# Pre-norm attention with level weights and a top-2 expert layer: two score groups of each head as one plain float32 product

## The reference

```
q = (x @ Wq.T).reshape(b, t, H, S)
k = (x @ Wk.T).reshape(b, t, H, S)
v = (x @ Wv.T).reshape(b, t, H, HD)
...
scores = jnp.einsum('bthd,bshd->bhts', q, k) * scale
...
A = scores * decay * lamw
y = jnp.einsum('bhts,bshd->bthd', A, v).reshape(b, t, H * HD)
out = y @ Wo.T + x
```

## Time and profile before

| what | value |
|---|---|
| median of three runs | 1522.22 us |
| the profiled execution's own time | 1523.29 us |
| its span, first to last instruction | 1521.5 us |
| TensorE busy | 1451.9 us, 95% |
| ScalarE busy | 1149.5 us, 76% |
| VectorE busy | 1013.6 us, 67% |
| GpSimd busy | 894.6 us, 59% |
| mean granted TensorE clock | 0.984 of full |

### The profile page before, as it was taken

How to read it: one execution, slowest core, us unless ns; L and a number is a source line. 1 busy time by engine, 2 the same in 40 slices (tenths; PEclk the granted TensorE clock), 3 DMA queues, 4 the chain that set the end, 5 groups by cost and what they waited for, 6 DMA issues and landing times.

```text
span 1521.5 us, 31013 instructions
## 1 busy us (share of the span) xinstructions
PE 1451.9 (95%) x10733; PEld 1198.0 (79%) x10733; DVE 1013.6 (67%) x2336; ACT 1149.5 (76%) x3379; POOL 894.6 (59%) x984
## 2 busy tenths in 40 slices
PE   5699999999999999999999999999999999999996
PEld 4488788878888788887888788887888878878873
DVE  5355756687656866577665876678766686657677
ACT  2588888787788778887787877888778877777730
POOL 2064558745596456945578455964569545685561
PEclk9699999999999999999999999999999999999998
DMA  6311111102010111101111011111111011111100
GB/s 186 63 11 17 40 17 31 14 16 48 9 37 17 23 38 38 17 8 38 25 38 14 16 36 18 38 17 23 38 38 16 9 26 21 39 17 17 23 8 15
DMA packets 256487, 44.14 MB, mean 29 GB/s; under 512 B 197976, under 2 KB 254666, under 8 KB 256202
## 3 DMA queue, kind: packets, MB, share of 16 engines
q1 hardware_dynamic: 255484, 41.90, 14.7%
q10 hardware_dynamic: 846, 0.25, 0.1%
HBM read 32.38 MB, written 9.18 MB: 27 GB/s over the span
## 4 chain that ended last, share of the span: by engine, by line
PE 61%; POOL 17%; DVE 9%; ACT 7%; issue 3%; SPq 1%; DMA 1%; ACTq 0%; POOLq 0%; DVEq 0%
PE o_ps L1344 16%; PE l_ps L1275 9%; POOL a_lo L603 7%; PE s_ps L1259 7%; PE s_ps L1261 6%; PE s_ps L1260 6%; PE aux L1259 5%; PE aux L1260 4%; PE aux L1261 4%; ACT w_all L727 3%; POOL e_rs L609 2%; DVE a_all L923 2%; POOL yn L628 2%; PE o_ps L1339 1%; POOL yn L638 1%
## 5 line engine op out<-in xcount | busy, mean ns | idle before, releaser
L603 POOL TENSOR_TENSOR a_lo<-a_all,a_hi 128x512 fp32r<-128x512 f32 (+2 forms) x640 | 710.8, 1127 | 561.0 <-ACT a_hi L749 560.3
L923 DVE TENSOR_TENSOR a_all<-s_ps,w_all 128x512 f32<-128x512 f32 (+3 forms) x768 | 421.8, 554 | 348.4 <-PE s_ps L1261 335.7
L727 ACT ACTIVATE w_all<-l_ps,bias 128x128 f32<-128x128 f32 x2304 | 628.9, 388 | 27.3 <-PE l_ps L1275 25.4
L749 ACT ACTIVATE a_hi<-a_all 128x512 fp32r<-128x512 f32 (+2 forms) x640 | 362.8, 598 | 210.2 <-DVE a_all L923 208.3
L1344 PE MATMUL o_ps<-a_hi,v_all 128*128 128x512 f32 (+2 forms) x1280 | 459.0, 363 | 7.2 <-POOL a_lo L603 7.2
L1259 PE MATMUL s_ps<-q_hi,xt_hi 128*128 128x512 f32 (+3 forms) x768 | 298.5, 389 | 9.5 <-DVE a_all L923 8.5
L1344 PEld LDWEIGHTS o_ps<-a_hi,v_all 128*128 128x128 f32 x1280 | 241.2, 188 | 45.5 <-issue 6.3
L1260 PE MATMUL s_ps<-q_lo,xt_hi 128*128 128x512 f32 (+3 forms) x768 | 266.5, 347 | 0.0
L1261 PE MATMUL s_ps<-q_hi,xt_lo 128*128 128x512 f32 (+3 forms) x768 | 266.4, 347 | 0.0
L1344 PE MATMUL o_ps<-a_lo,v_all 128*128 128x512 f32 (+2 forms) x640 | 230.0, 359 | 0.0
L1259 PEld LDWEIGHTS s_ps<-q_hi,xt_hi 128*128 128x128 f32 x768 | 145.7, 190 | 27.9 <-DVE a_all L923 19.8
(11 more groups left out here) (194 smaller groups left out, 2034.8 us busy)
## 6 DMA issues: line engine op xcount, KB each, us to landing
rb<-eb_scratch SPq DMA_DIRECT2D x1016, 0.8 KB
ra<-ea_scratch SPq DMA_DIRECT2D x512, 4.0 KB, 2.0
mt<-m_scratch SPq DMA_DIRECT2D x62, 128.0 KB, 2.1
nt<-n_scratch SPq DMA_DIRECT2D x62, 128.0 KB, 2.6
tx<-in_L_attn_x SPq DMA_DIRECT2D x9, 512.0 KB, 4.3
out<-yn SPq DMA_DIRECT2D x15, 256.0 KB, 2.8
yx<-in_L_attn_x SPq DMA_DIRECT2D x7, 512.0 KB, 4.2
ea_scratch<-tx SPq DMA_DIRECT2D x15, 128.0 KB
```

What stands on the lines that cost most here:

```text
L603: pool.tensor_tensor(a_lo[r][:, 0:t1 - t0], a[r][:, 0:t1 - t0], a_hi[r][:, 0:t1 - t0].bitcast(F32), ALU.subtract).then_inc(a_lo_done, 1)
L727: last = act.activation(w[k][:, W_AT[j] + dd, :].rearrange("p (f c) -> p f c", f=2), l_tiles[:, :, :, i - i0], ACT.Exp, bias=bias[b % 2][: ...
L749: act.activation(a_hi[r][:, 0:t1 - t0], a[r][:, 0:t1 - t0], ACT.Copy).then_inc(a_hi_done, 1)
L923: dve.tensor_tensor(a[(n * NG + g) % NA][:, 0:t1 - t0], s_ps[:, g % 2, 0:t1 - t0], w[n % 2][:, at:at + (t1 - t0) // P, :].rearrange("p i n ...
```

## The change

Groups 6 and 11 of each head, so 128 groups in all, are no longer three passes over split operands but one matmul of unsplit float32 tiles, as their values were already. For that, VectorE copies the last 128 columns of each half of the queries out of PSUM into `q_full`, between the two instructions of `take_q`, with a wait for its own copy. ScalarE copies the last 128 columns of each half of the transposed tokens into `x_full`, ahead of x_hi, and VectorE's `token_low` waits for that as well. The split tiles are still made for all columns. The size of one scratch area for DMA descriptors is set from 8192 to 4096 bytes.

```diff
+        q_full = [sb(f"q_full{k}", [P, 2 * P]) for k in range(2)]
+        x_full = [sb(f"x_full{k}", [P, 2 * P]) for k in range(2)]
...
+        q_full_done, x_full_done = sem("q_full_done"), sem("x_full_done")
...
                 def token_high(b, f):
...
                         act.wait_ge(y_done, 2 * (b - 1))
+                    act.activation(x_full[b % 2][:, f * P:(f + 1) * P], bank(("T", b, f))[:, HALF - P:],
+                                   ACT.Copy).then_inc(x_full_done, 1)
                     act.activation(xt_hi[b % 2][:, f * HALF:(f + 1) * HALF], bank(("T", b, f)), ACT.Copy).then_inc(t["hi"], 1)
...
                 def take_q(n, u):
...
                     dve.tensor_copy(q_hi[n % 2][:, cols], bank(piece)).then_inc(q_hi_done, 1)
                     dve.wait_ge(q_hi_done, Q_U * n + u + 1)
+                    dve.tensor_copy(q_full[n % 2][:, u * P:(u + 1) * P], bank(piece)[:, HALF - P:]).then_inc(q_full_done, 1)
+                    dve.wait_ge(q_full_done, Q_U * n + u + 1)
                     dve.tensor_tensor(q_lo[n % 2][:, cols], bank(piece), q_hi[n % 2][:, cols].bitcast(F32),
                                       ALU.subtract).then_inc(freed(piece), 1)
...
                 def token_low(b, f):
...
                     dve.wait_ge(t["hi"], 2 * b + f + 1)
+                    dve.wait_ge(x_full_done, 2 * b + f + 1)
...
                 def scores(n, g):
...
                     keys = slice(j * P, (j + 1) * P)
+                    if g in FULL:
+                        f = FULL.index(g)
+                        pe.matmul(s_ps[:, g % 2, 0:P], x_full[b % 2][:, f * P:(f + 1) * P],
+                                  q_full[k][:, f * P:(f + 1) * P], start=True, stop=True).then_inc(s_mm, 1)
+                        return
                     three(s_ps[:, g % 2, 0:t1 - t0], xt_hi[b % 2][:, keys], xt_lo[b % 2][:, keys],
                           q_hi[k][:, t0:t1], q_lo[k][:, t0:t1]).then_inc(s_mm, 1)
...
-    nc = bacc.Bacc("TRN2", target_bir_lowering=False, num_devices=1, dynamic_dma_scratch_size=8192)
+    nc = bacc.Bacc("TRN2", target_bir_lowering=False, num_devices=1, dynamic_dma_scratch_size=4096)
```

## The result

The changed kernel takes 1517.87 us (median of 13 runs, 1516.5 to 1519.85) against 1521.94 us for the kernel before (13 runs, 1520.55 to 1524.44). The ratio is 0.9976, with a 95% interval of 0.9967 to 0.9984: 4.1 us gained where 8 were forecast. The time lies inside the range of 1505 to 1521.5 us, but the gain is half of the forecast, so the account had a wrong term in it.

What follows compares the result with a forecast made beforehand. TensorE was taken to set the pace for some 60% of the time. 12.3 - 2.3 - 0.3 - 1.1 = 8.6 us off the profiled 1523.3 gave 1514.7, adjusted to the median as 1514 us against 1522.2, range 1505 to 1521.5.

Steps and rivals of the forecast that it cites:

- the size of the saving in a group: Groups 6 and 11 on TensorE: three narrow passes cost 0.41 us, the plain product 0.25, saving 0.16 (0.08 to 0.19).
- The range: Forecast time from 1505 to 1521.5 us, to reach the eaten gain and halfway to the case with every saving counted.
- the case where all counts: Rival: all 128 groups save 0.16 us, as GpSimd's and VectorE's work moves with TensorE; 1504 us, chance 0.10.
- 60% of the groups count: Only the 77 of 128 groups standing where TensorE sets the pace save time: 77 x 0.16 = 12.3 us.
- the fifth head's stretch: Part of each batch's chain paced by VectorE and ScalarE in turns, from 670.7 to 697.3 us: 26.6 us.
- The copies cost 2.3 + 0.3, with 1.1 for paths that come close: Seven exposed VectorE copies at 0.33 us, ScalarE's first at the start, and a tenth of the gain for new waits.
- The gain is eaten by waits: Rival: another 17 to 26 take_q exposed behind VectorE's copies lose 5.6 to 8.6 us; 1521 us, chance 0.16.
- VectorE becomes the bound: Rival: late q_lo holds its aux bank in every half head, all 126 copies exposed; 1552 us, chance 0.07.
- Four full passes: Rival: the plain float32 product costs four passes of 0.11 us, 0.50 a group instead of 0.41; 1533 us, chance 0.03.
- The scratch area: The smaller DMA descriptor scratch costs nothing; that it or something like it holds up loads had chance 0.02.
- The signs to look for: Trace: product 0.22 to 0.33 us, 128 copies near 285 ns, TensorE busy 15 to 20 us less, batch 178.1 us.
- the two signs of being wrong: TensorE's waits for take_q or weigh rising over 10 us, or the new product adding over 0.35 us to the chain.

Runs made afterwards that it cites:

- product_alone: The changed kernel without VectorE's 128-column copies for all heads but the first two, so later products read old queries: 1514.17 us, 0.9946 of the kernel before.
- copies_alone: The changed kernel with all copies made but groups 6 and 11 as three split passes again: 1526.56 us, 1.0025 of the kernel before.
- copy_twice: The changed kernel with VectorE's copy into q_full made twice over: 1530.74 us, 1.0050 of the kernel before.
- values_first: The changed kernel with the values of the group five back ahead of the scores in groups 6 and 11: 1520.05 us, 0.9981 of the kernel before.
- changed_again: The changed kernel itself, run again on another occasion beside the kernel before: 1519.13 us, ratio 0.9978.
- late_sum: The changed kernel with VectorE making q_full later, as q_hi + q_lo at places where it was idle, not inside take_q: 1516.38 us, 0.9962 of the kernel before.
- late_some: The changed kernel with q_full made later as q_hi + q_lo only for queries made in a batch's first and fifth heads: 1514.42 us, 0.9959 of the kernel before.

## Why the prediction was wrong

The step that failed is the size of the saving in a group: "The saving is 0.41 - 0.25 = 0.16 us for each group". It is 0.11, from 1.09 to 0.98 us in group 6 and from 0.63 to 0.52 in group 11. The two prices were read in different places. The 0.41 us of the three narrow passes stood behind the short float16 passes of l_ps, and the 0.22 to 0.27 us of the plain product stood behind wide float32r passes or narrow ones. Behind the float16 passes about 0.08 us is added to whatever comes next, and that goes to the product as well: 0.29, or 0.22 when it stands elsewhere; the three passes are 0.41, or 0.33 elsewhere. The prediction named the difference of place and took 0.25 anyway, though 0.29 and the 0.11 that follows lie inside its bounds (0.22 to 0.33, and a saving of 0.08 to 0.19). With 0.11 the sum is 77 x 0.11 = 8.5 instead of 12.3 us, and product_alone measured 8.7. The trace of the kernel before had the second price of the three passes already, behind transposes (line 1412) instead of float16 passes, 0.29 us where the rows of group 11 above have 0.36:

```profile
698.51 0.58 PE aux L1412 x4
699.08 0.07 PE s_ps L1259
699.15 0.11 PE s_ps L1260
699.26 0.11 PE s_ps L1261
```

The other steps:

- *The range.* Its lower end of 1505 is called halfway to the case where all counts (1504). From the forecast's own 1510 halfway would be 1507; nothing hangs on it.
- *60% of the groups count.* Right. Ten of 16 groups a batch at 0.11 us are the 1.1 us that product_alone shows (179.1 to 178.0). Inside the stretch that GpSimd paces nothing was gained: from 598.24 to 640.83 before and from 597.29 to 639.86 after, 42.6 us both times. "All of the saving counts" is refuted with that. (Of the 26.6 us counted as the fifth head's stretch, 1.5 were TensorE's, from 684.34 us on, which changes little.)
- *The copies cost 2.3 + 0.3, with 1.1 for paths that come close.* 3.7 us in all, and copies_alone measured 3.7. Put against product_alone the changed kernel loses more, 0.0030 of 1522 or 4.6 us. The sum was about right, and its parts weren't: it was not one take_q a batch at the full 0.33, but three on the chain that cost 0.66 us a batch together, 0.35 in the fifth head's stretch and the rest at the entry to GpSimd's list. The prediction missed the one in the first head. It checked the slack of TensorE's next scores (0.93 us in the earlier trace rows) and not that of GpSimd's list, which VectorE feeds as well. ScalarE's copy at the start cost 0.17 us, not 0.3: from ScalarE's first step there to xt_lo it is 0.63 us before and 0.80 after.
- *The gain is eaten by waits.* It would have needed 17 exposed take_q beyond the seven, and the 0.66 us a batch are worth some seven of them. But it was not what halved the gain: without any copies in the steady state the gain is 8.7 us, still short of the 12 that the prediction's terms give without them.
- *VectorE becomes the bound.* Not here. copy_twice shows how near it is: the second 0.3 us cost 11 us, 1.8 in a batch of the chain.
- *Four full passes.* Refuted by 0.29 us for the product where the rival needed 0.44 and more, and by 0.22 in values_first. The rule of the Trainium skill (FP8 and Floating Point Precision, TensorE Precision Notes) may still hold: 0.22 us is twice what one narrow float32r pass adds, and the trace, with two records for a call, can't say how many passes there are inside.
- *The scratch area.* Nothing, as said.
- *The signs to look for.* Two records with s_ps as output at 0.22 to 0.30 us, 128 copies of 292 ns and the wait of the weight loads for weigh (23.2 us, under 30) came as forecast. GpSimd's part is unchanged, but it is 42.6 us and not 45, since 3.3 of the 45.9 are ScalarE's. The batch was to take 178.1 us and takes 178.7. TensorE's busy time fell by 12 to 14 us (changed_again and product_alone, whose records are complete), not by 15 to 20, and its idle time rose by 4 to 5, not 8. Neither of the two signs of being wrong showed, though the gain was half of the forecast: they watched the waits and the product's own price, and not the difference to the passes that it replaced.

The 0.9 us between -5.0 (the sum of the parts) and -4.1 (the whole) lie inside the intervals, and the chain doesn't show them: by the table a batch is 1.12 us shorter with the product alone and 0.70 longer with the copies alone, -0.42 together, where the whole change gives -0.46. What stays open is why two copies more in the fifth head's stretch cost 1.2 us in copy_twice.

## What to carry to other kernels

Read the price of what goes and of what comes in the same neighbourhood: a delay that the instruction ahead causes falls on whichever comes next, and isn't saved with it. Before adding work to an engine that isn't the bound, check every consumer of what stands behind it in its list, not only the tightest one of the engine that is; work that can be done at any of several places belongs where that engine waits, and where it doesn't run beside another engine that sets the pace.

## What the runs showed of the hardware

- Behind a run of short float16 passes the next float32 or float32r pass comes about 0.08 us late, whichever it is (0.77 for 0.69 for wide values, 0.29 for 0.22 for the plain product, 0.35 for 0.28 for three narrow passes).
- A plain float32 product of 128 by 128 by 128 adds 0.22 us to the chain, two thirds of the 0.33 that three float32r passes of the same size take.
- A sum of two tiles out of its own memory took VectorE 281 ns for 128 columns in the median of late_sum (284 in late_some), where the copy from PSUM took 292 in the changed kernel. But 41 of the 126 sums of late_sum took 0.4 to 3.1 us, all of them beside a running GpSimd instruction. They end with it: the sum that starts at 97.05 us ends at 97.93, and the a_lo beside it at 97.78; the one from 575.33 ends at 576.22, its a_lo at 576.07. 36 of the short ones had a GpSimd instruction beside them too. GpSimd's step took 0.17 us more in the two places shown. No copy from PSUM did that: all 128 of the changed kernel took 291 to 293 ns.
